# Building an edge-count matrix: one side job moved between the two product blocks of a range, marks taken per range from PSUM, and range offsets as immediates

## The reference

```
z = h @ W.T + b
e = leaky_relu(concat([z[src], z[dst]]) @ aW.T + ab)
ex = exp(e - segment_max(e, dst)[dst])
out = segment_sum(ex / den[dst] * z[src], dst)
```

## Time and profile before

| | us |
|---|---|
| median of 3 runs | 4458.94 |
| lowest, highest | 4453.23, 4469.04 |
| profiled execution, span from first to last instruction | 4502.7 |
| profiled execution, own device time | not given |
| count build, within the span | about 225 to 1130 |
| attention layers | about 1140 to 2200 |
| edge, relation and convolution passes | the rest |

### The profile page before, as it was taken

How to read it: one execution, slowest core, us unless ns; L and a number is a source line. 1 busy time by engine, 2 the same in 40 slices (tenths; PEclk the granted TensorE clock), 3 DMA queues, 4 the chain that set the end, 5 groups by cost and what they waited for, 6 DMA issues and landing times. The chain is left out here.

```text
span 4502.7 us, 84639 instructions
## 1 busy us (share of the span) xinstructions
PE 3132.8 (70%) x29061; PEld 2437.5 (54%) x29061; DVE 3224.2 (72%) x7791; ACT 1435.4 (32%) x2737; POOL 1405.7 (31%) x1198
## 2 busy tenths in 40 slices
PE   0087777777238348158499985588888769959995
PEld 0054444444102112112499984287888769959995
DVE  7766666665489699699577763377767579967886
ACT  0034444444025125035399981233333200000000
POOL 0055555555264454554000000266666300000000
PEclk9978888888569679579699996599999879979997
DMA  8845555545458358267377740111111024413331
GB/s 323 322 129 143 153 144 148 157 131 149 147 172 264 114 166 263 88 200 246 106 221 221 222 148 12 56 24 23 24 23 24 14 67 111 109 28 102 88 91 47
DMA packets 413507, 587.19 MB, mean 130 GB/s; under 512 B 76420, under 2 KB 301787, under 8 KB 412709
## 3 DMA queue, kind: packets, MB, share of 16 engines
q1 hardware_dynamic: 366005, 447.98, 34.2%
q0 software_dynamic: 37728, 66.91, 5.5%
q10 hardware_dynamic: 9360, 66.90, 3.7%
HBM read 340.05 MB, written 234.93 MB: 128 GB/s over the span
## 5 line engine op out<-in xcount | busy, mean ns | idle before, releaser
L846 POOL DMA_INDIRECT slots<-bc_rec,idx x496 | 484.6, 977 | 410.4 <-ACT bc_rec L807 294.4
L1284 POOL DMA_INDIRECT rp_rows<-rel_rows,slot_rel x390 | 412.1, 1057 | 431.7 <-POOLq L118 182.3
L1106 PE MATMUL psum<-a_probs,z 128*65 128x512 f32 (+1 forms) x1050 | 445.7, 557 | 145.0 <-DVE a_probs L1039 145.0
L1320 DVE TENSOR_SCALAR rp_hot_src<-rp_key_rows,lane 128x384 bf16<-128x384 f16 x1560 | 383.5, 317 | 202.0 <-issue 88.5
L1534 PE MATMUL psum<-rel_pieces,rp_hot_src 128*128 128x192 bf16 x4680 | 452.1, 249 | 94.3 <-issue 75.8
L1074 ACT ACTIVATE a_tops<-a_tops,a_s_low 128x1024 f32<-128x1024 f32 (+2 forms) x300 | 284.1, 947 | 569.6 <-DVE a_tops L1030 569.1
L1534 PEld LDWEIGHTS psum<-rel_pieces,rp_hot_src 128*128 128x128 bf16 x4680 | 390.4, 99 | 128.8 <-issue 107.0
L483 POOL DMA_INDIRECT slots<-h,idx x192 | 327.6, 1706 | 352.3 <-DMA h<-recs 304.1
L1106 PEld LDWEIGHTS psum<-a_probs,z 128*65 128x65 f32 x1050 | 121.8, 137 | 469.4 <-DVE a_probs L1039 301.5
L703 DVE TENSOR_SCALAR bc_first_t<-bc_ramp,bc_key_t 128x128 f16<-128x128 f16 x500 | 136.5, 273 | 307.8 <-PE psum L729 172.7
L1030 DVE SCALAR_TENSOR_TENSOR a_tops<-table,a_s_rest,big 128x1024 f32<-128x1024 f32 (+2 forms) x300 | 309.3, 1031 | 32.8 <-DMA big<-shift_rows 32.8
(11 more groups left out here) (438 smaller groups left out, 6855.1 us busy)
## 6 DMA issues: line engine op xcount, KB each, us to landing
a_counts<-edge_counts SPq DMA_DIRECT2D x150, 512.0 KB
slots<-big ACTq DMA_DIRECT2D x65, 1005.0 KB
ep_rec<-slots SPq DMA_DIRECT2D x65, 1005.0 KB, 6.2
edge_counts<-bc_counts SPq DMA_DIRECT2D x12, 3125.0 KB
hot_rows<-ep_hot_src SPq DMA_DIRECT2D x325, 96.0 KB, 4.5
sp_hot_src<-hot_rows SPq DMA_DIRECT2D x325, 96.0 KB, 2.0
sq_hot_src<-hot_rows SPq DMA_DIRECT2D x325, 96.0 KB, 2.0
a_counts<-edge_counts SPq DMA_DIRECT2D x75, 282.5 KB
```

What stands on the lines that cost most here:

```text
L846: pool.indirect_dma_start(k.slots, bass.IndirectOffsetOnAxis(k.idx[:, first + t:first + t + 1], 0), rec[:, j, t, :], None).then_inc(scatte ...
L1106: last = nc.tensor.matmul(sums[:, a:b], k.z[:, s, 0:D + 1], probs[:, a:b], start=s == 0, stop=True, skip_group_check=True)
L1284: pool.indirect_dma_start(rows[:, n % ROW_SLOTS, s, 0:width], None, table, bass.IndirectOffsetOnAxis(k.slot_rel[:, at:at + 1], 0))\
L1320: last = v.tensor_scalar(hot_src[:, n % HOT_SLOTS, rel, :], key_rows[:, n % 2, :], k.lane[:, rel:rel + 1], None, ALU.is_equal)
```

## The change

Four things are changed in the count build and its preparation:

- PE issues the first side job of a range (`early_sides`, always a record job, 0 to 4) between the `first` and the `more` products; the others (`late_sides`) stay behind `more`. ACT takes the early job before it copies the range's counts. Where a range has no late job (ranges 2 to 4 of the first group), PE waits for its own `more` products and reports `summed` itself.
- ACT makes the sign of a range right after its copy, from the same PSUM banks, and `evacuated` is reported after both. The 128 x 3125 sign per group is gone.
- `above` has two buffers that alternate by group. The second is the memory of `z`, which is first used by the attention layers. The semaphore `above_ready` is replaced by `evacuated`.
- The offset of the range is an immediate of L704 instead of a per-partition scalar; the table, its index ramp and its conversion are gone.

```diff
@@ edge_keys
-                g.iota(ramp_i[:, :], pattern=[[1, COLS]], base=0, channel_multiplier=0)
-                g.iota(base_i[:, :], pattern=[[-COLS, NWIN]], base=0, channel_multiplier=0).then_inc(made, 1)
+                g.iota(ramp_i[:, :], pattern=[[1, COLS]], base=0, channel_multiplier=0).then_inc(made, 1)
...
-                v.tensor_copy(base_s[:, :], base_i[:, :])
@@ build_counts
-        counts, above = sb("counts", [P, 2, NT, 2 * GROUP]), sb("above", [P, NT, GROUP], FP16)
+        counts = sb("counts", [P, 2, NT, 2 * GROUP])
+        spare = k.z[:, :, :].rearrange("p t c -> p (t c)").bitcast(FP16)[:, 0:NT * GROUP]
+        above = [sb("above", [P, NT, GROUP], FP16)[:, :, :], spare.rearrange("p (t c) -> p t c", c=GROUP)]
...
+        def early_sides(g, w):
+            return sides(g, w)[0:1]
+        def late_sides(g, w):
+            return sides(g, w)[1:]
@@ DVE, one_hots
-                        last = v.tensor_scalar(to_s[:, u, :], ramp[:, :], column(key_s, t), column(base_s, j),
+                        last = v.tensor_scalar(to_s[:, u, :], ramp[:, :], column(key_s, t), -float(COLS * j),
                                                ALU.subtract, ALU.is_equal)
@@ PE
-                    pe.wait_ge(above_ready, g + 1)
+                    pe.wait_ge(evacuated, (g + 1) * GROUP_WIN)
...
                     products(y, first_s, first_t, True, first_used)
+                    for x in early_sides(g, w):
+                        side(g, x)
                     before = blocks()
                     with pe.Fori(0, steps) as i:
                         pe.wait_ge(more_ready, before + i)
                         pe.sem_inc(fence, 1)
                         products(y, more_s, more_t, False, more_used)
                     nc.regs_add(done, done, steps)
-                    if not sides(g, w):
+                    if not late_sides(g, w):
                         pe.wait_ge(more_used, before + steps)
                         pe.sem_inc(summed, 1)
-                    for n, x in enumerate(sides(g, w)):
...
+                    for n, x in enumerate(late_sides(g, w)):
+                        side(g, x, n == 0)
@@ ACT
-                    nc.scalar.activation(count_cols(g)[:, :, w * WIN:(w + 1) * WIN],
-                                         ps[(g * GROUP_WIN + w) % PS_SETS].rearrange("p (t c) -> p t c", c=WIN),
-                                         ACT.Copy)\
-                        .then_inc(evacuated, 1)
+                    found = ps[(g * GROUP_WIN + w) % PS_SETS].rearrange("p (t c) -> p t c", c=WIN)
+                    at = slice(w * WIN, (w + 1) * WIN)
+                    nc.scalar.activation(count_cols(g)[:, :, at], found, ACT.Copy)
+                    nc.scalar.activation(above[g % 2][:, :, at], found, ACT.Sign).then_inc(evacuated, 1)
...
-                def find_above(g):
-                    act.wait_ge(evacuated, (g + 1) * GROUP_WIN)
-                    nc.scalar.activation(above[:, :, :], count_cols(g), ACT.Sign).then_inc(above_ready, 1)
...
                     for w in range(GROUP_WIN):
+                        for x in early_sides(g, w):
+                            take_side(g, x)
                         take_window(g, w)
-                        for x in sides(g, w):
...
-                    find_above(g)
+                        for x in late_sides(g, w):
+                            take_side(g, x)
```

More of the change, by code:

```diff
@@ L512, in load_marks, with edge_keys @@
         sp.dma_start(self.marks_now[:, at, :], by_group[:, at, :]).then_inc(self.marks_in[y], 16)
-def edge_keys(k, att, key_s, key_t, base_s, ramp, win_bounds):
+def edge_keys(k, att, key_s, key_t, ramp, win_bounds):
     nc, d = k.nc, k.dram
@@ L535, in edge_keys @@
         pair_i, row = sb("pair_i", [P, 1], INT32), sb("row", [1, 3, NWIN])
-        ramp_i, base_i = sb("ramp_i", [P, COLS], INT32), sb("base_i", [P, NWIN], INT32)
+        ramp_i = sb("ramp_i", [P, COLS], INT32)
         src_i, dst_i = sb("src_i", [P, ET], INT32), sb("dst_i", [P, ET], INT32)
@@ L621, in build_counts @@
         key_s, key_t = sb("key_s", [P, ET + PAD_TILES]), sb("key_t", [P, ET + PAD_TILES])
-        base_s = sb("base_s", [P, NWIN])
         ramp, win_bounds = sb("ramp", [P, COLS], FP16), sb("win_bounds", [1, NWIN], INT32)
-        edge_keys(k, att, key_s, key_t, base_s, ramp, win_bounds)
+        edge_keys(k, att, key_s, key_t, ramp, win_bounds)
         sem = ctx.enter_context(semaphores(nc, "bc"))
@@ L628, in build_counts @@
         more_ready, more_used = sem("more_ready"), sem("more_used")
-        summed, evacuated, above_ready, fence = sem("summed"), sem("evacuated"), sem("above_ready"), sem("fence")
+        summed, evacuated, fence = sem("summed"), sem("evacuated"), sem("fence")
         ident_ready = sem("ident_ready")
@@ L747, in turn_marks @@
                     a, b = MARK_CHUNKS[i]
-                    pe.wait_ge(above_ready, g + 1)
+                    pe.wait_ge(evacuated, (g + 1) * GROUP_WIN)
                     pe.wait_ge(side_taken, job - 1)
                     for t in range(a, b):
-                        last = nc.tensor.matmul(k.psum[0:GROUP, bank, (t - a) * P:(t - a + 1) * P], above[:, t, :],
-                                                ident[:, :], start=t == a, stop=True, skip_group_check=True)
+                        last = nc.tensor.matmul(k.psum[0:GROUP, bank, (t - a) * P:(t - a + 1) * P],
+                                                above[g % 2][:, t, :], ident[:, :], start=t == a, stop=True, skip_group_check=True)
                         if mark_sum and t == a:
@@ L755, in turn_marks, with side @@
                     last.then_inc(side_done, 1)
+                def side(g, x, mark_sum=False):
+                    if x < PRE_JOBS:
+                        edge_products(g, x, mark_sum)
+                    else:
+                        turn_marks(g - 1, x - PRE_JOBS, *side_job(g, x), mark_sum)
                 pe.wait_ge(ident_ready, 1)
@@ L772, in _ @@
                     nc.regs_add(done, done, steps)
-                    if not sides(g, w):
+                    if not late_sides(g, w):
                         pe.wait_ge(more_used, before + steps)
                         pe.sem_inc(summed, 1)
-                    for n, x in enumerate(sides(g, w)):
-                        if x < PRE_JOBS:
-                            edge_products(g, x, n == 0)
-                        else:
-                            turn_marks(g - 1, x - PRE_JOBS, *side_job(g, x), n == 0)
+                    for n, x in enumerate(late_sides(g, w)):
+                        side(g, x, n == 0)
                 for i in range(NMARK):
@@ L816, in take_marks, with take_side @@
                         .then_inc(side_taken, 1)
-                def find_above(g):
-                    act.wait_ge(evacuated, (g + 1) * GROUP_WIN)
-                    nc.scalar.activation(above[:, :, :], count_cols(g), ACT.Sign).then_inc(above_ready, 1)
+                def take_side(g, x):
+                    if x < PRE_JOBS:
+                        take_rec(g, x)
+                    else:
+                        take_marks(g - 1, x - PRE_JOBS, *side_job(g, x))
                 nc.scalar.preload_act_table(ACT.Copy)
@@ L824, in _ @@
                     for w in range(GROUP_WIN):
+                        for x in early_sides(g, w):
+                            take_side(g, x)
                         take_window(g, w)
-                        for x in sides(g, w):
-                            if x < PRE_JOBS:
-                                take_rec(g, x)
-                            else:
-                                take_marks(g - 1, x - PRE_JOBS, *side_job(g, x))
-                    find_above(g)
+                        for x in late_sides(g, w):
+                            take_side(g, x)
                 for i in range(NMARK):
```

1 line of the change is left out of this document (removed).

## The result

The changed kernel takes 4464.61 us (median of 20 launches), the kernel before beside it 4453.60 us (20 launches): a ratio of 1.0023, 95% interval 1.0014 to 1.0031. That is 11 us slower by measurement, and within the 0.3% that the prediction called no difference. It lies above the forecast of 4424 us and above the range, which ended at 4462 us.

The account below looks back on a forecast made before the run. It took POOL's cycle of four scatters plus a 2.41 us wait for ACT's record copy to bound the count build; -34 us (early job) and -0.5 us, rounded to -35, gave 4459 - 35 = 4424 us, range 4315 to 4462.

Parts of the forecast that it names:

- The baseline: Whole kernel: durations from the 4502.7 us profiled execution, saving carried over as it is to the unprofiled median of 4458.94 us.
- The early job: Count build: ACT finds the record first in line, POOL's wait falls from 2.41 to 2.13 us, 34 us less.
- the slower rival: Count build: ACT's Sign moves onto the path at ranges with three or more side jobs; up to 4489 us; chance 0.10.
- Sign per range: ACT in the count build: 88 us instead of 70.6, lying in POOL's burst, so nothing on the path.
- The upper bound of 87 us: Sign per range on ACT: the cost at 0.7 us a range if the cover were gone.
- The immediate: DVE, L704: about 373 instead of 444 ns, 70 us of DVE time, nothing on the path; bounds 0 and 70.
- the end of the build: Last group's marks: ready sooner, but ACT waits for the previous marks' store to land; nothing, +-1 us.
- The habit after the burst: Count build: side jobs issued in a burst's second half are seen complete only about 1.1 us after the burst.
- The PE rival: Count build: PE's chain sets the pace, POOL only follows; 5.9 instead of 7.2 us a range, 159 us less; chance 0.20.

Follow-up runs that it names:

- after: The changed kernel with all four parts of the change, against the kernel before: 4464.61 us, ratio 1.0023.
- group_sign: Changed kernel with one Sign per group from the copied counts, as before; early job and immediate stay: 4453.16 us, 0.9989 to the kernel before.
- sign_last: Changed kernel with each range's Sign made from the SBUF counts behind the late side jobs: 4451.00 us, 0.9986 to the kernel before.
- after_again: The changed kernel, unchanged, on chip 1, where the kernel before took 4168.9 us: 4138.05 us, 0.9937.
- none_before: Kernel before without the count build's 496 scatters and ACT's waits for them, one more zero fill: 4252.30 us, 0.9540.
- b_again: The kernel before, unchanged, run and profiled once more on chip 7: 4453.94 us, 0.9995.

## Why the prediction was wrong

**The baseline.** The step "the durations are those of the profiled execution, whose span is 4502.7 us ... I carry the saving over as it is" took the POOL wait at 2.41 us. A repeat has 2.32 (276.6/119), and after has 2.29 (268.3/117). Of the 44 us between the two spans 16 are in this stage, 19 in the relation pass. The wait that the forecast was to shrink was 18 us longer than in the repeat (294.4 against 276.6), so half of the 34 us was an excess of that one execution over the median, from which the saving was then subtracted. That alone would have left a forecast of about 4440 us.

**The early job.** This is the step that failed: "The wait goes from 2.41 to 2.13 us", 34 us less. POOL's wait came to 2.29 us in after, and to 2.18 in group_sign, where the Sign is out of the way and the early job was still worth only 2.8 us by the medians. In after, ranges 0 to 3 gained 0.35 us each on average, which looks like the 0.28 predicted, but ranges 1 and 2 have this gain only where range 4 is long, so the likeness is luck in part. Why they lose it with a short range 4 is open; their granted clock falls with it (at range 1 from 0.98 in after to 0.86 in group_sign and 0.76 in sign_last). The assumption that the next early job always comes in the second half of the burst failed at range 4. The prediction had found the place, "only range 3 of each group (three late jobs) should wait, 24 x 0.7 = 17 us", but as the slower rival with 0.10, with the sum to be made over 92 waits. The wait itself was sized well: PE's idle time ahead of mark jobs grew by 0.71 us in this cycle. The cycle grew by 1.41 us, because PE was also busy 1.1 us longer, at a granted clock of 0.63 instead of 0.86; for the clock the prediction had only 0.05 us a range. Had the 17 us been subtracted in the sum, the forecast would have been 4441; with the measured 1.41 x 24 = 34 us, 4458.

**Sign per range.** This is the second term that failed. "It lies in the POOL burst", and so 88 us of ACT for nothing, was wrong: 31 us in the old order, 11 (against group_sign) to 13 (against sign_last) in the new, 15 to 16 by the ratios. Its duration was right; its place ahead of the late jobs, on an engine 42% busy, was what cost. The upper bound of 87 us held.

**The immediate, the buffers, the end of the build.** Nothing, as said. 380 ns against the estimate of 373. PE still waits for a Sign at the end, the last range's, 1.48 us in place of 3.30, but the store's landing decides as before, at 5.67 us in place of 3.23:

```profile
1105.65 0.82 PEld L758 LDWEIGHTS psum<-bc_ident,bc_above 128*125 128x125 f16 x7 [1.48 <-ACT bc_above L806]
1106.02 0.28 SPq L882 DMA_DIRECT2D edge_marks<-bc_marks  x1
...
1111.59 0.98 ACT L826 ACTIVATE bc_marks<-psum 125x512 uint8<-125x512 f32 x2 [5.67 <-DMA edge_marks<-bc_marks]
```

**The habit after the burst** was read rightly from the earlier trace rows and served in the sum as a constant. It is real, and the scatters, with which it goes, are the largest thing in this build (186 us). But one chip does not have it. There the forecast's number is met (31 us less against 35), by luck: POOL waits 43.8 us in all for ACT's record in after_again, so a wait of 2.41 us that falls to 2.13 isn't what was saved.

**The PE rival** (0.20), "POOL only follows it", did not hold on the chips with holds: with POOL's scatters gone and PE's work unchanged, the range takes 5.34 us instead of 7.0, so POOL does not only follow. Its 5.9 us a range were within reach, but by fewer scatters and not by the order of side jobs, and at a granted clock of 0.98. The rule of the Trainium skill that stood beside it (TensorE: Matmul & The Clock Gate, section "HAM oscillation — how this bites in real kernels"), that idle gaps lower the clock, agrees between these two: PE idles 100 of the 675 us in none_before and 151 in b_again, at 0.98 and 0.85. The sum of the idle time is not enough to tell the clock, though: after idles 128 us there and has 0.81.

## What to carry to other kernels

Work a sum from a profiled execution whose own time is near the median, and where it is not, ask first which stage holds the excess. Where work moves behind or ahead of a fixed list of side jobs, make the sum for each place in the list: a mean over ranges hid a gain of 1.41 us and a loss of 1.41 us a group. Look at the granted clock for each place too. An instruction on a half idle engine need not be free where others wait for what comes behind it; moving the Sign behind the late jobs, with the third scatter paced by PE's progress, gave a ratio of 0.985 where the kernel before takes 4458 us (the change alone 1.002) and took it from 0.994 to 0.988 on chip 1. Measure a change of this size on more than one chip.

## What the runs showed of the hardware

- On the chips where the kernel before takes 4450 us or more PE's completions reach the others late while POOL issues indirect DMAs: 167 of 624 in b_again, 241 of 669 in after, and on the chip of 4169 us 6 of 769. VectorE's and ScalarE's completions are not late (0 of 174 and 0 of 222 in b_again). Taking the scatters away takes 186 us of the stage's 774; from the one kind of chip to the other the relation pass goes from 660 to 529 us. The Trainium skill (Perfetto Trace Analysis, section "DMA Instruction — SWDGE (GPSIMD)") says that such a record ends when the descriptors are made, not when the data has moved. No run here shows what still goes on in the 1.1 us behind the fourth record. PE goes on starting matmuls meanwhile (all 71 cases in b_again); whether the products or only their report are late wasn't separated, nor why one chip is free of it.
- The hold does not grow evenly with the scatters: two a range cost 30 us, four 186 us, and a pause of 0.85 us in the middle doesn't help (1.0041 on chip 7).
- A 625-column one-hot with a second per-partition scalar takes 444 ns, with an immediate in its place 380 ns.
- PE's granted clock from 225 to 900 us is 0.98 without scatters, 0.95 with half, 0.85 with all, and 0.81 in after, with the same scatters in another order. Within after its mean by place goes from 0.63 at range 4 to 0.98 at range 1.
